# A two-layer metaformer on one core: routing and experts of the first layer in two programs, or in one that is interleaved

## The reference

```
x = x + conv0(norm over channels of x)         # 7x7 depthwise
t = x as tokens                                 # 9216 x 128
n = layernorm(t)
logits = n @ Wg                                 # 8 experts
top 2 logits, weights = softmax of the two
t = t + sum over the 2 experts of weight * (silu(n @ W1[e]) @ W2[e])     # 128 -> 512 -> 128
x = x + conv1(norm over channels of x)          # up by 2, leaky, down by 2
t = t + a second layer of 8 gated experts of width 256, top 2
```

## Time and profile before

| | us |
|---|---|
| median of the runs | 1513.65 |
| the profiled execution | 1519.82 |
| its span, first to last instruction | 1517.7 |
| routing stage, from about 156 to 417 | 261 |
| first experts, from about 417 to 753 | 336 |

### The profile page before, as it was taken

The page is one execution under the profiler, slowest core; times in us unless marked ns, Lnnn a source line. Parts: engine busy times, 40 slices in busy tenths (PEclk is TensorE's granted clock), DMA queues, the critical chain, the costliest instruction groups (busy, mean ns, idle before and its releaser), DMA issues. The chain is left out here.

```text
span 1517.7 us, 28287 instructions
## 1 busy us (share of the span) xinstructions
PE 1118.1 (74%) x6195; PEld 880.7 (58%) x6196; DVE 979.3 (65%) x3803; ACT 646.2 (43%) x1295; POOL 733.0 (48%) x703
## 2 busy tenths in 40 slices
PE   0599134431099999999739979889889599999920
PEld 0599133321089999999626546455555478888820
DVE  6766166657056666666466676767775688888844
ACT  2465145532034444444333564555655444444410
POOL 0332177778534444444352265454663765665620
PEclk9999555555599999999959999989989699999965
DMA  9242585411122222222161022021110233333359
GB/s 225 58 113 65 147 259 93 79 49 51 36 67 63 62 62 63 62 64 62 46 180 29 14 57 58 22 64 41 28 31 20 71 98 83 87 85 85 87 137 260
DMA packets 138877, 123.73 MB, mean 82 GB/s; under 512 B 65813, under 2 KB 119310, under 8 KB 137408
## 3 DMA queue, kind: packets, MB, share of 16 engines
q1 hardware_dynamic: 107149, 72.91, 19.7%
q0 software_dynamic: 19968, 39.44, 8.3%
q10 hardware_dynamic: 11667, 10.46, 2.5%
HBM read 72.74 MB, written 51.06 MB: 82 GB/s over the span
## 5 line engine op out<-in xcount | busy, mean ns | idle before, releaser
L645 POOL DMA_INDIRECT routed<-r_xn,r_slot x320 | 339.8, 1062 | 285.2 <-DVEq L634 162.3
L1020 POOL DMA_INDIRECT answers<-e_y,e_dest x152 | 145.8, 959 | 199.0 <-ACT e_y L1140 194.0
L1424 PE MATMUL c_pz<-c_c,down 116*120 116x512 f32 (+1 forms) x392 | 197.1, 619 | 0.0
L1020 POOL DMA_INDIRECT answers<-c_c x152 | 145.9, 960 | 90.8 <-issue 68.6
L1192 DVE COPY e_ht<-e_ps_ht 128x512 f32<-128x512 f32 x152 | 105.2, 692 | 121.6 <-PE e_ps_ht L1061 121.6
L1071 PE MATMUL e_ps_y<-w,e_ht 128*128 x1216 | 160.6, 275 | 0.0
L1398 PE MATMUL c_py<-c_xh,gl 121*116 121x512 f32 (+1 forms) x196 | 123.6, 631 | 33.2 <-DVE c_xl L1527 29.6
L1071 PEld LDWEIGHTS e_ps_y<-w,e_ht 128*128 128x128 f32 x1216 | 147.8, 192 | 0.1
L1537 DVE SCALAR_TENSOR_TENSOR c_c<-c_a 116x1024 f32<-116x1024 f32 (+1 forms) x60 | 76.6, 1277 | 69.1 <-ACT c_a L1482 67.7
L1135 ACT ACTIVATE e_h<-e_ps_h 128x512 f32<-128x512 f32 x154 | 92.0, 598 | 57.8 <-PE e_ps_h L1053 57.8
L1482 ACT ACTIVATE c_a<-c_py 116x512 f32<-116x512 f32 x116 | 68.5, 590 | 105.1 <-PE c_py L1398 102.2
(11 more groups left out here) (206 smaller groups left out, 2915.2 us busy)
## 6 DMA issues: line engine op xcount, KB each, us to landing
answers<-answers SPq DMA_DIRECT2D x32, 480.0 KB, 5.9
e_xg<-routed SPq DMA_DIRECT2D x159, 66.0 KB, 1.8
c_c<-routed SPq DMA_DIRECT2D x159, 66.0 KB, 1.8
c_w<-in_w SPq DMA_DIRECT2D x26, 393.8 KB
routed<-r_xn,r_slot POOLq DMA_INDIRECT x320, 2.4
c_x<-in_xh SPq DMA_DIRECT2D x4, 1170.0 KB, 11.1
w1l<-in_w SPq DMA_DIRECT2D x2, 2048.0 KB, 10.4
out<-x ACTq DMA_DIRECT2D x16, 240.0 KB
```

The lines of the kernel that those rows point to most:

```text
L645: ro.nc.gpsimd.indirect_dma_start(ro.xs, bass.IndirectOffsetOnAxis(ap=ro.slot[0:px, q, c:c + 1], axis=0), ro.xn[0:px, q, k, t, :], None).t ...
L1020: ex.nc.gpsimd.indirect_dma_start(ex.ys, bass.IndirectOffsetOnAxis(ap=ex.dest[:, s:s + 1], axis=0), ex.y[:, s, :], None).then_inc(ex.store ...
L1424: ins = nc.tensor.matmul(ps_z[q % 3][0:rows, :], r.down[0:PPX, m * TPX:m * TPX + rows], c[0:PPX, p % R, :], start=p == ROWS * q, stop=p == ...
```

## The change

The two stages become one, `route0_expert0_phase`, fully written out on every engine.

- Six groups (`BEFORE`) are routed ahead of the blocks, as is the turn and logits of the seventh. The other 14 are worked on between the blocks: group g starts at step `PICK[g]`, one group every 7.5 blocks, from step 0 to step 97. Its normalise, copies, turn and logits come up to 5 steps ahead, its ranks, place and scatters up to 4 steps behind.
- The table comes in eight parts (`PARTS`): after 3, 5, 8, 10, 13, 15, 18 and 20 groups, with 15, 29, 50, 65, 86, 101, 123 and 152 blocks listed. The blocks that a part lists are full for any data. SP waits for a part and for its groups' scatters before it loads the part's first block; the blank tails are written by SP ahead of block 123.
- PE reads the expert of each block by its own register load, no longer packed; the table has the expert times 512.
- POOL's queue has for each block one scatter to `answers`, and behind four of them two scatters each of a group (`first_scatter`).
- SP issues the loads of 10 groups, then the expert weights, then the other 50 loads, and only then the first block. The filters' factors are loaded at block 101 and worked on at steps 119 to 121.
- Roots are taken for groups in five batches (`BATCHES`) with kept statistics. The two weights come from a tanh of half the gap on ACT, in place of exponential, sum, reciprocal and product. ACT, not DVE, normalises and fills in the destination, which is now a float that DVE converts when a block is read. The weights of the experts are split in eight pieces each, between groups 2 and 5.
- x's and y's PSUM share two banks, so the second product also waits for a later block's split. The waits on `stored` for a slot of the block 8 before stay. The hardware loops, the beats and the barrier between the two stages are gone.

```diff
+BEFORE = 6
+PARTS = ((3, 15), (5, 29), (8, 50), (10, 65), (13, 86), (15, 101), (18, 123), (GROUPS, BLOCKS))
+assert all(blocks <= sure_blocks(n) for n, blocks in PARTS[:-1])
+BATCHES = ((0, 1), (1, 5), (5, 9), (9, 14), (14, GROUPS))
...
+def parts_count(tb, dve, ch, k, counts):
+    nc, last = tb.nc, k == len(PARTS) - 1
+    need(dve, tb.counted, k + 1)
+    if last:
+        nc.vector.tensor_tensor(tb.tail_i[:], counts, tb.r.region[0:1, 0:EXPERTS], ALU.add).then_inc(tb.tail_ready, 1)
+    nc.vector.tensor_scalar(tb.n_i[:], counts, float(P - 1 if last else 0), None, ALU.add).then_inc(tb.count_read, 1)
+    need(dve, tb.count_read, k + 1)
+    ch.after(nc.vector.tensor_scalar(tb.n_i[:], tb.n_i[:], 7, None, ALU.arith_shift_right))
+    ch.after(nc.vector.tensor_copy(tb.n[:], tb.n_i[:]))
...
+def first_measure(ro, dve, g):
+    nc, px, q = ro.nc, pixels(g % QT), g % QT
+    need(dve, ro.x_in[g], 16 * CGS)
+    if g == 0:
+        dve.wait_ge(ro.cleared, 3)
+    need(dve, ro.spread, g - 1)
+    for t in range(IG):
+        ins = nc.vector.bn_stats(ro.stats[0:px, g % 2, t, :], ro.r.x[0:px, g, t, :])
+    ins.then_inc(ro.measured, 1)
...
+def first_root(ro, act, k):
+    begin, end = BATCHES[k]
+    need(act, ro.var_ready, k + 1)
+    ro.nc.scalar.activation(ro.std[0:TPX, begin:end, :], ro.std[0:TPX, begin:end, :], ACT.Sqrt).then_inc(ro.std_ready, 1)
...
+def first_half(ro, act, g):
+    px = pixels(g % QT)
+    need(act, ro.gap_ready, g + 1)
+    ro.nc.scalar.activation(ro.half[0:px], ro.gap[0:px], ACT.Tanh, scale=-0.5).then_inc(ro.half_ready, 1)
...
+def first_place(ro, dve, ch, g):
+    nc, px, q = ro.nc, pixels(g % QT), g % QT
+    need(dve, ro.rank_ready, g + 1)
+    nc.vector.tensor_tensor(ro.earlier[0:px], ro.earlier[0:px], ro.group_sum[0:px], ALU.add)
+    ch.after(nc.vector.tensor_tensor(ro.rank[0:px], ro.ranks(g), ro.r.region[0:px], ALU.add))
+    rank = ro.rank[0:px].rearrange("p (t e) -> p t e", e=EXPERTS).unsqueeze(2).to_broadcast([px, IG, 2, EXPERTS])
+    ch.after(nc.vector.tensor_tensor(ro.prod[0:px], ro.onehot[0:px], rank, ALU.mult))
+    need(dve, ro.half_ready, g + 1)
+    ro.slot_free(dve, g)
+    for k, sign in enumerate((0.5, -0.5)):
+        nc.vector.tensor_scalar(ro.xn[0:px, q, k, :, WEIGHT], ro.half[0:px], sign, 0.5, ALU.mult, ALU.add)
+    ch.after(nc.vector.tensor_reduce(ro.slot_f[0:px], ro.prod[0:px].rearrange("p t k e -> p (t k) e"), AX.X, ALU.add))
+    nc.vector.tensor_copy(ro.slot[0:px, q], ro.slot_f[0:px]).then_inc(ro.slot_ready, 1)
...
+def first_logits(ro, tb, pe, g):
+    px = pixels(g % QT)
+    need(pe, ro.xnt_ready, g + 1)
+    need(pe, ro.picked_ready, g)
+    if g >= BEFORE:
+        need(pe, ro.slot_ready, g)
+        need(pe, tb.count_read, sum(n <= g for n, _ in PARTS))
...
+def block_load(ex, sp, b):
+    slot = b % ex.U
+    start = sp.value_load(ex.r.table[0:1, 0, b:b + 1], min_val=0, max_val=EXPERTS * REGION + (SPARE - 1) * P)
+    need(sp, ex.x_split, b - ex.U + 1)
+    sp.dma_start(ex.xg[:, slot, :], ex.xs[bass.ds(start, P), :]).then_inc(ex.x_in[slot], 16)
...
+def block_split(ex, dve, b):
+    nc, i, slot = ex.nc, b % 2, b % ex.U
+    need(dve, ex.x_turned, b + 1)
+    need(dve, ex.h_ready, b - 1)
+    need(dve, ex.stored[slot], 16 * (b // ex.U))
+    nc.vector.tensor_copy(ex.xh[:, i, :], ex.ps_x(b)).then_inc(ex.hi_done, 1)
+    nc.vector.tensor_copy(ex.dest[:, slot:slot + 1], ex.xg[:, slot, DEST:DEST + 1])
+    nc.vector.tensor_copy(ex.weight[:, slot:slot + 1], ex.xg[:, slot, WEIGHT:WEIGHT + 1])
+    need(dve, ex.hi_done, b + 1)
+    nc.vector.tensor_tensor(ex.xl[:, i, :], ex.ps_x(b), ex.xh[:, i, :].bitcast(F32), ALU.subtract).then_inc(ex.x_split, 1)
...
+def block_second_product(ex, pe, b, w):
+    need(pe, ex.ht_ready, b + 1)
+    need(pe, ex.x_split, min(b + 4, BLOCKS))
+    if b + 4 >= BLOCKS:
+        need(pe, ex.y_ready, b - 1)
+    for c in range(FF // P):
...
+        PICK = {g: (15 * (g - BEFORE)) // 2 for g in range(BEFORE, GROUPS)}
+        AHEAD = ex.AHEAD
+        MEASURE = {g: n * 5 // 2 for n, g in enumerate(range(BATCHES[2][1], GROUPS))}
+        VARIANCE = {k: MEASURE[end - 1] + 2 for k, (_, end) in enumerate(BATCHES) if k > 2}
+        FACTORS = PARTS[-2][1] - 4
...
+            def load(b):
+                for k in range(len(PARTS)):
+                    if b == first_of(k):
+                        begin_part(k)
+                block_load(ex, sp, b)
+            def begin_part(k):
+                sp.wait_ge(tb.ready, 2 * (k + 1))
+                if k == len(PARTS) - 1:
+                    sp.wait_ge(tb.tail_ready, 1)
+                    for e in range(EXPERTS):
+                        end = sp.value_load(tb.tail_i[0:1, e:e + 1], min_val=0, max_val=EXPERTS * REGION - P)
+                        sp.dma_start(xs[bass.ds(end, P), :], r.blank[:, e, :]).then_inc(tails, 16)
+                for q in range(QT):
+                    need(sp, ro.scattered[q], 16 * CHOICES * len(range(q, PARTS[k][0], QT)))
+                if k == len(PARTS) - 1:
+                    sp.wait_ge(tails, 16 * EXPERTS)
+            for ig in range(2):
+                load_x(ig)
+            weights_load(wt, sp, io, 0, w_in)
+            for ig in range(2, IMAGE_GROUPS):
+                load_x(ig)
+            for b in range(AHEAD):
+                load(b)
+            for s in range(BLOCKS):
+                if s + AHEAD < BLOCKS:
+                    load(s + AHEAD)
+                if s == PARTS[-3][1]:
+                    load_factors()
...
+            for s in range(BLOCKS):
+                if s:
+                    block_answer(ex, act, s - 1)
+                if s + 2 < BLOCKS:
+                    block_activate(ex, act, s + 2)
+                for k in at(VARIANCE, s, 1):
+                    first_root(ro, act, k)
+                for g in at(PICK, s, 2):
+                    first_half(ro, act, g)
+                for g in at(PICK, s, -3):
+                    first_copy_turned(ro, act, g)
+                for g in at(PICK, s, -4):
+                    first_copy_rows(ro, act, g)
+                for g in at(PICK, s, -5):
+                    first_normalise(ro, act, g)
...
+            for b in range(BLOCKS):
+                block_scatter(ex, pool, b)
+                for n in range(CHOICES // 2):
+                    for g in at(PICK, b, 1 + n):
+                        first_scatter(ro, pool, g, 2 * n)
+                        first_scatter(ro, pool, g, 2 * n + 1)
...
+            pe.wait_ge(tb.ready, 2)
+            for b in range(2):
+                weights(b)
+            for b in range(2):
+                block_turn_x(ex, pe, b)
+            pe.wait_ge(w_low, EXPERTS)
+            for b in range(2):
+                block_first_product(ex, pe, b, w[b])
+            block_turn_x(ex, pe, 2)
+            for s in range(BLOCKS):
+                block_turn_h(ex, pe, s)
+                if s + 3 < BLOCKS:
+                    block_turn_x(ex, pe, s + 3)
+                if s:
+                    block_second_product(ex, pe, s - 1, w[s - 1])
+                if s + 2 < BLOCKS:
+                    for k in range(1, len(PARTS)):
+                        if s + 2 == first_of(k):
+                            pe.wait_ge(tb.ready, 2 * (k + 1))
+                    weights(s + 2)
+                    block_first_product(ex, pe, s + 2, w[s + 2])
+                for g in at(PICK, s, 2):
+                    first_ranks(ro, pe, g)
+                for g in at(PICK, s, 4):
+                    if part_after(g) is not None:
+                        first_count(ro, tb, pe, part_after(g))
+                for g in at(PICK, s, -2):
+                    if g > BEFORE:
+                        first_logits(ro, tb, pe, g)
+                for g in at(PICK, s, -4):
+                    first_turn(ro, pe, g)
...
+            for g in range(BEFORE):
+                pick(g)
+                if g == 0:
+                    first_scale(ro, dve, ch, 1)
+                first_place(ro, dve, ch, g)
+                if part_after(g) is not None:
+                    table(part_after(g), 0)
+                if g < 2:
+                    for n in range(BATCHES[2][0] + 2 * g, BATCHES[2][0] + 2 * g + 2):
+                        first_measure(ro, dve, n)
+                        first_spread(ro, dve, n)
+                    if g == 1:
+                        first_variance(ro, dve, 2)
+                elif g == 2:
+                    first_scale(ro, dve, ch, 2)
+                elif g == 3:
+                    for n in range(4):
+                        table(0, 1 + n)
+                for e in range(EXPERTS):
+                    if 2 + e // 2 == g:
+                        low_w(e)
...
+            for b in range(3):
+                block_split(ex, dve, b)
+            for s in range(BLOCKS):
+                block_copy_turned(ex, dve, s)
+                if s + 3 < BLOCKS:
+                    block_split(ex, dve, s + 3)
+                if s < 4:
+                    table(1, 1 + s)
```

(66 more changed lines are left out.)

462 lines of the change are left out of this document (310 added, 152 removed).

## The result

| | before | after |
|---|---|---|
| median of the runs, us | 1514.01 (1511.8 to 1516.83, 4 runs) | 1449.22 (1448.47 to 1449.25, 4 runs) |
| span of the profiled execution | 1517.7 | 1447.3 |
| end of POOL's last scatter of the experts | 752.3 | 679.2 |

The ratio is 0.956, 95% interval 0.954 to 0.958. The forecast was 1432, in a range of 1412 to 1468: the time went the way and by the mechanism of rival A, but the gain is 17 us short of the sum.

What follows compares the result with a forecast made beforehand. POOL bound routing and PE the experts, each leaving the other idle. Group 6's first rows at 291.9, thirteen 20.3 us periods and a tail end the stage at 670.6, 81.7 us sooner: 1432 us, range 1412 to 1468.

Steps and rivals of the forecast that it cites:

- rival A: The forecast itself: POOL's period bounds the steps with groups, 1432 us, with its own bounds 1416 to 1446; chance 0.57.
- Start: Ahead of the first block: SP's load queue, through at 269.6, sets the start; first turn at 276, step 0 at 280.4.
- POOL as the new bound: Steps 0 to 101, with 14 groups: POOL needs 19.85 us per group against PE's 17.75; period taken as 20.3.
- the two stalls nearly cancel: Mixed steps: POOL's idling up to 2.8 us for a group's place and its lag holding DVE and PE nearly offset each other.
- Register load "I take 0": PE's new register load in each step is hidden behind queued matmuls: 0 us, the other end 0.76 each.
- Behind it nothing is changed: After the expert stage, conv1 starts from the same barrier with the same data, so the 81.7 us gain stays whole.
- The step from profile to median: Profiled execution forecast at 1438.1 us; the old one stood 6.2 above the median of the runs, hence 1432.
- B: Rival: PE's register loads are not hidden; 0.76 us each gives 1512, half of it 1457; chance 0.12.
- C: Rival: PE's granted clock falls to the lower level when it waits for POOL in mixed steps, up to 1630 us; chance 0.05.
- D: Rival: ACT and DVE latency, table loads if tanh and silu share no table, 1446 to 1468; 0.20 with late SP or lock.
- The lock on the shared port: DVE's instructions hold POOL's port; statistics in mixed steps cost at most 3 us per group, 1471; 0.20 with D or late SP.
- E: Rival: blocks wait for their part of the table, 2.65 us per step; called unlikely and small, others 0.01.

Runs made afterwards that it cites:

- experiment 6: The changed kernel with all twenty groups routed ahead of the blocks (`BEFORE = 20`), undoing only the overlap: 1524.16 us, ratio 1.003 to 1.007 to before.
- experiment 10: The changed kernel with SP loading x before the expert weights, and the last 25 pieces of x during steps 0 to 24: 1428.3 us.
- Experiment 4: The changed kernel with one row scatter behind each of eight blocks' scatters, from block PICK+3, instead of two behind each of four: 1433.24 us.
- experiment 1: The changed kernel with PE reading the expert only for every eighth block, so most blocks get another expert's weights: 1441.17 us.
- Experiment 2: The changed kernel with PE's register load for block s + 3 at the end of step s, behind the preceding first product: 1439.62 us.

## Why the prediction was right, and where 17 us were missed

- **Two engines, one idle in each stage: right.** Undoing the overlap alone (experiment 6) gives back 81 us at the stage's end.
- **Start: right, by two errors that cancel in part.** The first turn was forecast at 276 and came at 274.9. SP was through 1.9 us late (the loads at 0.87 and the wait at 7.2 us were near the 0.86 and 10 of the sum), but the 3 us for standing behind the last x loads did not show. That SP sets the start is seen in PE's wait of 9.45 us and shown by experiment 10. Step 0's first product was at 280.2; the forecast's 280.4 is for its turn, and 1.35 us from there to the product (424.74 - 423.39 before) makes 281.7: 1.6 us sooner than forecast. The wait for the weights came a group sooner than the text has it, ahead of group 2, and left POOL free at 281.9 and not at 275 to 278; that did not move the blocks.
- **POOL as the new bound: right in kind.** From step 0 to step 100 the sum had 271.0 us and the trace has 278.5. Of these 7.5, 4.1 are in the thirteen periods (268.0 us between the first rows of groups 6 and 19, 20.6 each, against 263.9), the other 3.3 ahead of them: from step 0's product to group 6's first rows it took 13.5 and not 10.2 us. The failed step is "the two stalls nearly cancel": 20.3 us a period was chosen near the low end of 19.85 to 22.65. Bursts make POOL late, PE stops, the next place comes late, POOL stops; both were paid. Experiment 4, with the rows spread and begun later, is down at POOL's own need. What the sum did not have is that a scatter lands late beside the loads of the factors (6.8 us and not 2.3), and that the clock falls behind a longer stall: the four products behind the falls came 3.3 to 4.7 us after the one ahead, some 5.6 us more than four steps of 2.3, which is an estimate of what the low clock cost PE and not of what reached the end. PE was busy for 93% of the mixed part, 19.2 us a period and not 17.75, and waited for splits some 1.2 us a group and not 2.5; 7.5 register loads are 0.75 us of the difference.
- **Register load "I take 0": wrong.** The bounds were 0 and 0.76; it is 0.10 (experiment 1; and 2.24 against 2.14 without the factors' steps). The reason given, that two loads in eight steps left no bump, did not carry over: there the loads stood elsewhere. Experiment 2 shows that position decides. From step 100's first product to step 149's it was 114.1 us: 49 x 2.14 = 104.9, 4.9 for the loads, 4.3 for the last burst and the factors (forecast 5.7). POOL's end comes 6.5 us later: 120.6. The sum had 670.6 - 551.4 - 1.35 = 117.9 for it all.
- So the stage's end: 280.2 + 278.5 + 120.6 = 679.2, against 281.7 + 271.0 + 117.9 = 670.6: -1.6 start, +7.5 mixed, +2.7 tail.
- **A's lower bound** is 1432 - 14 = 1418 and not 1416; nothing hangs on it.
- **"Behind it nothing is changed": wrong by 2.7 us.** The end of the stage costs 5.8 us more (cause open; semaphore count excluded). conv1 and the rest took 756.1 us against 759.2, which hides half of it. In other runs, with the same code there, they took 752.3 (experiment 6) to 758.6 (10), so this half is chance of the execution.
- **The step from profile to median: wrong by 6 us.** The old profiled execution stood 6 above the median and I took the same for the new one; the new one (1449.25) stands on its median. This is luck of the executions profiled, not a cost. The 17.2 us are 8.6 + 2.7 + 5.9.
- **Rivals.** B is there, at 0.10 of its 0.76 us. C did not come as told, 0.97 is the mean clock of the mixed part; in small it is there, four falls to the lower level behind PE's longest waits. D: tanh shares silu's table, and even exp's loads are free. The lock on the shared port cost nothing visible in the mixed part: scatters beside statistics took 0.93 to 1.0 us, as in the earlier trace rows. Beside the factors' operations, where POOL has time to spare, three took 2.13 to 2.54. E did not occur.

## What to carry to other kernels

When two stages with different bounds are merged, the merged part costs what its busiest queue needs (here 1.26 and 1.30 us an instruction on POOL) only if that queue's work is spread evenly; a burst brings both engines to the edge of their slots, where they wait in turn. Look also at what else moves bytes then: here, in eight of the eleven interleaved runs, DVE's longest wait stood beside 2.8 MB of loads that no block needed. No run moved them, so what that would give is not known. Put a register load where it has a whole step of queued work ahead of its use, not just ahead of the instruction that uses it. Once the merge is done, the next thing to look at is what is issued ahead of the first merged step: here 18 us lay in the order of one load queue.

## What was not expected of the hardware

- A table load on ACT is 1.28 us, and 28 more of them in 280 us moved nothing in this kernel.
- The granted clock of PE has a mean of 0.97 when PE is busy for 93% of the time, but behind waits of 1.6 to 3.7 us it fell to 0.50, for some 3 to 6 us each.
- A scatter of 128 rows lands in 2.3 us and took 6.8 beside 2.8 MB of loads on another queue, with the DMA engines at 0.99.
- A register load on PE cost nothing measurable behind the first product, 0.10 us just ahead of it, and a second one there 0.32.
- The idle time between stages is 6.2 to 6.6 us in two kernels and 11.5 to 12.2 in the others, and 40 semaphores are not why.
